# A mixture of 16 experts: sorting the token rows by a scatter, and gathering them by an inverse permutation

## The chip, the core and the metric

The kernel runs on one core of one Trainium2 chip. The metric is the device time of one launch in microseconds (us); several runs are taken and their median is compared. Engines are named as the profile names them: PE is TensorE (PEld its weight loads), ACT ScalarE, DVE VectorE, POOL GpSimd, SP SyncE, which issues most DMA transfers here.

## What is computed

The program is a decoder of four layers on `x` of 4 x 256 tokens by 256 (1024 tokens), with attention, cross attention and an MLP in each. The change lies in the MLP of the third layer, a mixture of 16 experts of which each token takes 4, with a shared expert beside them:

```python
def _L2_ffn_ref(hidden_states, router_w, w_gate, w_up, w_down, sh_gate, sh_up, sh_down, sh_gate_w):
    E, K = (16, 4)
    I_MOE, I_SH = (176, 704)
    h = hidden_states.reshape(-1, orig[-1])          # 1024 x 256
    probs = jax.nn.softmax(h @ router_w.T, axis=-1)
    top_vals, top_idx = jax.lax.top_k(probs, K)
    top_vals = top_vals / jnp.maximum(top_vals.sum(-1, keepdims=True), 1e-09)
    comb = jnp.zeros((N, E), h.dtype).at[jnp.arange(N)[:, None], top_idx].add(top_vals)
    g = jnp.einsum('nh,ehi->eni', h, w_gate)
    u = jnp.einsum('nh,ehi->eni', h, w_up)
    y = jnp.einsum('eni,eih->enh', jax.nn.silu(g) * u, w_down)
    routed = jnp.einsum('enh,ne->nh', y, comb)
    shared = jax.nn.silu(h @ sh_gate) * (h @ sh_up) @ sh_down
    sg = jax.nn.sigmoid(h @ sh_gate_w)
    return routed + sg * shared
```

`h` is the layer-normalised `x`, and the result is added to `x`.

## The kernel before

Tokens lie on 128 partitions in `TT` = 8 tiles, in `X`; features are turned into columns in `HT` for products. The whole stage is the function `experts2`. Each engine has its own program, and semaphores order them; within an engine the order of the source is the order of execution.

**Head.** VectorE and ScalarE normalise (`norm_steps`), writing `HX`, whose rows hold 256 features and 16 more columns. TensorE turns them, multiplies by the router's weights (L2160), and works on the shared expert. That one is cut into six units of 128 hidden columns (`NSH` = 6; the last is half empty), each in two chunks `c` of 512 tokens: `go_up(i, c)` (L2091, gate and up halves), a Silu on ScalarE (L2203), a product on VectorE (`mult`, L2250), `go_down(i, c)` (L2101), which accumulates in four PSUM banks. `FRONT` = 5 units are done ahead of the experts and one behind. Weights of the units come in a ring of four, the last two loaded by SP at L2051.

VectorE meanwhile softmaxes the logits and ranks them. It compares all pairs of the 16 probabilities of a token in `C1` and `C2`, 8 x 16 x 16 = 2048 elements per partition (L2287 to L2294), `RK` is the number of greater ones and `MASK` says `RK` < 4 (L2297). TensorE counts with triangular and all-one matrices how many tokens each expert has before this one (`count`, L2109 to L2114). From the counts come `NB`, the blocks of 128 rows of each expert, `FIRST`, its first block, and `SLOT`, the row of each of the 4 x 8 x 128 token choices in a sorted table (L2327). The number of blocks is fixed at `NBLK` = 47, with padding. `EXPERT` names the expert of each block (L2340).

**Sorting.** POOL scatters the rows of `HX` by `SLOT` into `sorted_rows` in DRAM, in 32 indirect transfers of 128 rows of 1088 bytes (L2379). The table was filled with zeros long before (`late_loads`, L260), so padding rows are zeros. The 16 extra columns carry, per expert, where the result has to go.

**The loop over 47 blocks.** SP loads the 128 rows of block `b` (L2047) and its expert's weights in three transfers, 384, 128 and 64 KB (L2035, L2041, L2043), in rings of four. Its order per block is: rows, a register load of the expert's number, a wait for the up-projection four blocks back, the up weights, a wait for the down-projection four blocks back, the down weights. TensorE runs `turn(b+2)` (two transposes, L2122), `expert_up(b+1)` (six products, L2132) and `expert_down(b)` (two products, L2144). ScalarE copies the turned rows (L2209) and takes the Silu (L2215), VectorE multiplies (`hidden`, L2257 and L2258), finds the destinations from the extra columns (`destination`, L2263 and L2265) and copies the result out of PSUM (`evacuate`, L2271). POOL scatters the result by `DEST` to `chosen` in DRAM, a row for each of the four choices of each token (L2384); rows of padding lie out of bounds and are skipped. In every other block VectorE also quantises a piece of the last layer's ternary weights (`replace`, L2612 and L2613).

**Tail.** The last shared unit; SP loads `chosen` back in 16 transfers (L2075), and VectorE adds the four rows of each token with their weights to `X`, 32 instructions (L2368).

## Time and profile before

| | |
|---|---|
| median of 3 runs | 1313.59 us (1309.03 to 1316.88) |
| the profiled execution | 1310.13 us, span 1308.4 us |
| mean granted TensorE clock | 0.942 |
| TensorE busy | 1129.7 us (86%) |
| VectorE busy | 818.6 us (63%) |
| ScalarE busy | 563.0 us (43%) |
| GpSimd busy | 340.4 us (26%) |
| moved by DMA | 80.83 MB |

A share of busy time is a mean over all stages of the four layers. The stage of the change runs from 805.65 to 1066.4 us of the span, and its own limits are read from the windows and the timeline of that stretch. "Idle before" in a row is the time in which the engine stood, with what released it; a row with xN merges N instructions, and its length runs from the first start to the last end.

### The profile page before, as it was taken

Reading aid. Unit: us, or ns where it says so; the run is one execution under the profiler, and the core shown is the slowest. Engines: PE = TensorE matmul, PEld = TensorE weight load, DVE = VectorE, ACT = ScalarE, POOL = GpSimd, SP = SyncE. Lnnn points to the kernel's source line nnn. Section 1 sums busy time; section 2 is a strip of 40 time slices with the busy share of each in tenths; the row PEclk is TensorE's granted clock in tenths of the full one; section 3 lists DMA queues with packets and bytes.
Section 4 is the critical chain, followed back from the end, with each engine's and each line's share of the span. In section 5 each row is a group of like instructions: output and inputs, shape, how many; then the busy total and the mean of one; then the engine's idle time right before and its main releaser. Section 6 shows DMA issues by size and latency. Waiting matters only on the chain. (4 is left out here: it accounts for less than half of the span.)

```text
span 1308.4 us, 25171 instructions
## 1 busy us (share of the span) xinstructions
PE 1129.7 (86%) x9501; PEld 714.9 (55%) x9516; DVE 818.6 (63%) x2375; ACT 563.0 (43%) x1145; POOL 340.4 (26%) x401
## 2 busy tenths in 40 slices
PE   5888899879999899899999899885888859995898
PEld 3456544447754534456666454555776625663455
DVE  6733487566777444667886674643554376879855
ACT  3667234653434433354443554411222215446443
POOL 2444203100003100145554132073333304451100
PEclk9888899889999899999999999797999969997999
DMA  9000000000074030000000000055888630000000
GB/s 384 3 2 2 1 2 1 1 1 1 1 278 134 1 130 0 1 2 3 3 3 2 2 2 1 13 187 157 263 275 265 186 127 1 2 3 1 1 1 33
DMA packets 44874, 80.83 MB, mean 62 GB/s; under 512 B 5634, under 2 KB 33994, under 8 KB 43985
## 3 DMA queue, kind: packets, MB, share of 16 engines
q1 hardware_dynamic: 40960, 70.55, 16.5%
q0 software_dynamic: 3792, 8.66, 1.8%
q8 instruction: 76, 1.25, 0.4%
q14 instruction: 46, 0.37, 0.1%
HBM read 62.91 MB, written 18.24 MB: 62 GB/s over the span
## 5 line engine op out<-in xcount | busy, mean ns | idle before, releaser
L863 ACT ACTIVATE PT<-PS 128x384 f32<-128x384 f32 (+1 forms) x320 | 153.2, 531 | 185.7 <-PE PS L676 138.2
L272 PE MATMUL PS<-identb 128*128 128x512 bf16 x420 | 106.9, 394 | 19.4 <-PEq L2031 14.8
L796 DVE CUSTOM_DVE_ANT_0 junk<-PS,TRI 128x128 bf16<-128x128 f32 (+1 forms) x384 | 112.7, 353 | 3.9 <-PE PS L657 0.2
L657 PE MATMUL PS<-KS,QM 32*128 32x128 f32 (+1 forms) x768 | 86.7, 347 | 7.5 <-DVE QM L830 6.6
L835 DVE RECIPROCAL OD<-OD 128x256 f32<-128x256 f32 x40 | 69.9, 1747 | 30.9 <-ACT OD L871 25.9
L676 PE MATMUL PS<-QM,KS 32*128 32x256 f32 (+1 forms) x768 | 88.5, 347 | 0.0
L914 POOL TENSOR_TENSOR OD<-OD 128x256 f32<-128x256 f32 x24 | 17.4, 725 | 271.0 <-DVE OD L835 271.0
L904 POOL TENSOR_SCALAR_AFFINE_SELECT PT<-PT 128x512 f32<-128x512 f32 x96 | 60.6, 635 | 98.7 <-ACT PT L863 98.7
L657 PEld LDWEIGHTS PS<-KS,QM 32*128 32x128 f32 x768 | 65.6, 184 | 30.2 <-DVE QM L830 16.6
L272 PEld LDWEIGHTS PS<-identb 128*128 128x128 bf16 x420 | 39.9, 102 | 69.3 <-issue 34.6
L2384 POOL DMA_INDIRECT chosen<-YB,DEST x47 | 48.9, 1040 | 102.7 <-DVE YB L2271 99.9
L745 PE MATMUL PS<-PT,CST 128*32 128x256 f32 (+1 forms) x1280 | 75.4, 353 | 0.0
L2132 PE MATMUL PS<-XT,WE 128*128 128x128 f32 x564 | 72.5, 280 | 0.0
L2132 PEld LDWEIGHTS PS<-XT,WE 128*128 128x128 f32 x564 | 68.5, 196 | 0.4 <-ACT XT L2209 0.4
L676 PEld LDWEIGHTS PS<-QM,KS 32*128 32x128 f32 x768 | 65.6, 184 | 1.9 <-issue 1.2
L1151 POOL TENSOR_TENSOR ROT<-RC,RS 128x512 f32<-128x512 f32 x16 | 20.3, 1270 | 169.6 <-DVE RS L1140 168.3
L745 PE MATMUL PS<-PT,VM 128*32 128x256 f32 (+1 forms) x1024 | 58.3, 345 | 2.0 <-POOL PT L904 1.8
L2257 DVE TENSOR_TENSOR HD<-PS,AE 128x128 f32<-128x128 f32 x47 | 13.7, 291 | 68.1 <-ACT AE L2215 67.8
L1967 DVE SCALAR_TENSOR_TENSOR HB<-HA,ROW,GB 128x512 f32<-128x512 f32 x40 | 30.1, 751 | 40.5 <-ACT HA L1902 36.1
L2122 PE MATMUL PS<-CST,XB 128*128 128x128 f32 x94 | 20.6, 304 | 37.3 <-DMA XB<-sorted_rows 36.9
L2209 ACT ACTIVATE XT<-PS 128x256 f32<-128x256 f32 x47 | 18.0, 383 | 80.7 <-PE PS L2122 80.5
L1902 ACT ACTIVATE HA<-PS,VEC 128x512 f32<-128x512 f32 x42 | 28.7, 687 | 53.5 <-PE PS L1829 53.5
(374 smaller groups left out, 2688.8 us busy)
## 6 DMA issues: line engine op xcount, KB each, us to landing
WE<-w2e_in SPq DMA_DIRECT2D x47, 384.0 KB, 3.9
sorted_rows<-NOTHING SPq DMA_DIRECT2D x1, 6392.0 KB, 35.9
XB<-sorted_rows SPq DMA_DIRECT2D x47, 136.0 KB, 3.7
WE<-w2e_in SPq DMA_DIRECT2D x47, 128.0 KB
WA<-wl_in SPq DMA_DIRECT2D x1, 5137.0 KB, 15.2
GB<-gate_rows SPq DMA_DIRECT2D x8, 512.0 KB, 5.2
WB<-wb_in SPq DMA_DIRECT2D x1, 3208.0 KB, 19.2
WE<-w2e_in SPq DMA_DIRECT2D x47, 64.0 KB
```

The source lines that it names most:

```text
L272: pe.matmul(PS[:, bank, :].rearrange("p (a n) -> p a n", a=4), identb[:], identb[:].rearrange("p (a n) -> p a n", a=1).to_broadcast([P, 4, ...
L657: return pe.matmul(PS[:, s, m * T:m * T + n], queries(U, v)[rows, m * P:(m + 1) * P], keys(U, v)[rows, 0:n], start=True, stop=True, skip_g ...
L676: last = pe.matmul(bank, keys(U, v)[rows, n * P:(n + 1) * P], queries(U, v)[rows, lo:hi], start=n == 0, stop=r > 1, skip_group_check=True, ...
L745: last = pe.matmul(PS[at:at + 32, 7, what * T + lo:what * T + hi], lhs, src, start=what == 0 and v == 0 and n == 0, stop=v == r - 1 and n ...
L796: last = dve.tensor_tensor_reduce(junk[:, s, m * P:m * T + P], PS[:, s, m * T:m * T + (m + 1) * P], TRI[:, (1 - m) * P:T], 1.0, NEG, ALU.a ...
L835: dve.reciprocal(o, o).then_inc(S["at_inv"], 1)
L863: act.activation(PT[:, g % 3, st_slot(k), 0:W], PS[:, st_bank(g, k), 0:W], ACT.Exp, scale=scale).then_inc(S["at_exp"], 1)
L904: pool.affine_select(v, v, [[0, 4], [1, P]], ALU.is_ge, 0.0, base=0, channel_multiplier=-1).then_inc(S["at_masked"], 1)
L1902: act.activation(HA[:, n % 4, :], PS[:, n % 2, :], ACT.Gelu, bias=b).then_inc(S["act_out"], 1)
L1967: ins = dve.scalar_tensor_tensor(HB[:, n % 4, :], HA[:, n % 4, :], gelu_b1[:, f:f + 1], GB[:, owner[f], c * CH:(c + 1) * CH], ALU.subtract ...
L2132: last = pe.matmul(up_bank(b)[:, i * P:(i + 1) * P], WE[:, b % RINGE, (i * KD + k) * P:(i * KD + k + 1) * P], XT[:, b % 2, k * P:(k + 1) * ...
L2384: pool.indirect_dma_start(chosen, bass.IndirectOffsetOnAxis(DEST[:, b:b + 1], 0), YB[:, b % RINGE, :], None, bounds_check=SPARE_ROW - 1, o ...
```

## The change

- **Ranks.** `C1` and `C2` go. The probabilities lie in `PRX`, rows of 16 with four -1 behind. `max` gives the eight largest of a token (8 instructions), the lower four are overwritten by -1, `match_replace` writes -2 where one of the upper four stands (8 instructions), and `MASK` is where the result differs. The four choices of a token are no longer in order of size but of expert: a running sum over `MASK` gives each choice a label from 1 to 32.
- **Inverse permutation.** Slot numbers are split into block and place in the block. `INB` says for each of the 32 choices of a partition in which block it is (32 x 47), `INR` in which place (32 x 128, bf16, in the memory of `RET1`). Two copies of `INB`, multiplied by `code` (POOL) and `row` (ScalarE), are `CODE`. 32 products on TensorE (`locate`) sum `INR` by `CODE`, which gives for each place of each block the number of its row (`DEST`) and of its token (`FROM`).
- **Gather.** SP writes the normalised tokens to `token_rows` in DRAM once. POOL gathers the 128 rows of a block by `FROM`, six blocks ahead (`RINGX`), between its scatters. `sorted_rows`, the 32 scatters, the clearing write and `destination` go.
- **Weights.** One transfer of 576 KB per block, five blocks ahead (`RINGW`). The last 48 hidden rows of an expert lie twice in `HD`, once for each half of the output, so that their down weights fill 128 partitions; `expert_down` has three products and `hidden` three.
- **Order.** `FRONT` is 3 instead of 5. The router's product is cut in two. The ternary sums of ScalarE move into blocks 1 to 12, the scales behind block 17, the replacements to blocks 18 and on. Shared unit 5 has both halves in one PSUM bank, so that its up-projection is half as long.

```diff
-        FRONT = 5
-        COUNT_AT = 1
+        FRONT = 3
+        PAIRS = TT * TOP2
...
                 def _(sp):
-                    for i in range(RING2, NSH):
-                        sp.wait_ge(S["down_ps"], d["down_ps"] + NCH * (i - RING2 + 1))
+                    def weights(b):
+                        e = sp.value_load(EXPERT[0:1, b:b + 1], min_val=0, max_val=E2 - 1)
+                        sp.dma_start(WE[:, b % RINGW, :], w2e[bass.ds(e, 1)].rearrange("a p n -> p (a n)")
+                                     ).then_inc(S[f"weights{b % RINGW}"], 16)
+
+                    for g in range(TT // 2):
+                        norm["tokens"](sp, g)
+                        sp.dma_start(token_rows[2 * g * P:2 * (g + 1) * P, :].rearrange("(t p) n -> p t n", p=P), H[:, 2 * g:2 * g + 2, :]
+                                     ).then_inc(S["rows_kept"], 16)
+                    for i in range(RING2, min(NSH, RING2 + FRONT - 1)):
+                        sp.wait_ge(S["down_ps"], d["down_ps"] + units(i - RING2, NCH - 1))
                         sp.dma_start(W2[:, i % RING2, :], w2s[i]).then_inc(S[f"w_slot{i % RING2}"], 16)
                     sp.wait_ge(S["blocks"], d["blocks"] + 1)
...
-                    for b in range(RINGE, NBLK):
-                        sp.wait_ge(S["turned"], d["turned"] + b - RINGE + 1)
-                        sp.wait_ge(S["row_of"], d["row_of"] + b - RINGE + 1)
-                        rows(b)
-                        e = sp.value_load(EXPERT[0:1, b:b + 1], min_val=0, max_val=E2 - 1)
-                        sp.wait_ge(S["up_ps"], d["up_ps"] + routed(b - RINGE))
-                        up_weights(b, e)
-                        sp.wait_ge(S["down_ps"], d["down_ps"] + routed(b - RINGE))
-                        down_weights(b, e)
+                    for b in range(RINGW):
+                        weights(b)
+                    for b in range(NBLK - RINGW):
+                        sp.wait_ge(S["down_ps"], d["down_ps"] + routed(b))
+                        weights(b + RINGW)
...
+                    def locate(pe):
+                        pe.wait_ge(S["weighed"], d["weighed"] + 1)
+                        pe.wait_ge(S["coded"], d["coded"] + 1)
+                        pe.wait_ge(S["built"], d["built"] + 2)
+                        for j in range(PAIRS):
+                            last = pe.matmul(PS[:, 3, 0:2 * NBLK], INR[:, j, :], CODE[:, j, :], start=j == 0, stop=j == PAIRS - 1)
+                        last.then_inc(S["located"], 1)
...
-                    L(dve.tensor_tensor(C1[:], theirs, mine, ALU.is_gt))
-                    scales(dve, PS[:, 5, :])
-                    L(dve.tensor_tensor(C2[:], theirs, mine, ALU.is_equal))
+                    for t in range(TT):
+                        last = dve.max(TOPV[:, t, :], PRX[:, t, 0:E2])
+                    L(last)
...
+                    for t in range(TT):
+                        last = dve.match_replace(LEFT[:, t, :], TOPV[:, t, :], PRX[:, t, :], -2.0)
...
+                    dve.tensor_tensor(INB[:], WHERE[:, 1].rearrange("p (j b) -> p j b", b=1).to_broadcast([P, PAIRS, NBLK]),
+                                      cst("count")[:, 0:NBLK].rearrange("p (j b) -> p j b", j=1).to_broadcast([P, PAIRS, NBLK]),
+                                      ALU.is_equal).then_inc(S["placed"], 1)
+                    residents(0)
+                    mult(1, 1)
+                    residents(1)
...
                 def _(pool):
-                    pool.memset(HD[:], 0.0)
-                    pool.memset(WE[:, :, UP + D:W2N], 0.0).then_inc(S["blank"], 1)
-                    pool.wait_ge(S["slots"], d["slots"] + 1)
-                    pool.wait_ge(S["rows_clear"], d["rows_clear"] + 16)
-                    for t in range(TT):
-                        for k in range(TOP2):
-                            pool.indirect_dma_start(sorted_rows, bass.IndirectOffsetOnAxis(SLOT[:, t, k:k + 1], 0), HX[:, t, :], None
-                                                    ).then_inc(S["rows_sent"], 16)
+                    def gather(b):
+                        j = b % RINGX
+                        if b >= RINGX:
+                            pool.wait_ge(S["turned"], d["turned"] + b - RINGX + 1)
+                        pool.indirect_dma_start(XB[:, j, :], None, token_rows, bass.IndirectOffsetOnAxis(FROM[:, b:b + 1], 0)
+                                                ).then_inc(S[f"x_slot{j}"], 16)
...
+                    for b in range(RINGX):
+                        gather(b)
                     for b in range(NBLK):
-                        pool.wait_ge(S["row_of"], d["row_of"] + b + 1)
                         pool.wait_ge(S["evacuated"], d["evacuated"] + b + 1)
                         pool.indirect_dma_start(chosen, bass.IndirectOffsetOnAxis(DEST[:, b:b + 1], 0), YB[:, b % RINGE, :], None,
                                                 bounds_check=SPARE_ROW - 1, oob_is_err=False).then_inc(S[f"out_slot{b % RINGE}"], 16)
+                        if b + RINGX < NBLK:
+                            gather(b + RINGX)
```

How TensorE comes from the shared units to the blocks, before (`WA` holds the units' weights, `XB` a block's rows, `WE` its expert's):

```order
L2091 MATMUL PS<-HT,WA 128x512 x4
L2101 MATMUL PS<-WA,MO 128x256 x12
L2122 MATMUL PS<-CST,XB 128x128 x4
L2132 MATMUL PS<-XT,WE 128x128 x6
L2122 MATMUL PS<-CST,XB 128x128 x2
L2132 MATMUL PS<-XT,WE 128x128 x6
L2144 MATMUL PS<-WE,HD 128x256 x2
```

The same place in the changed kernel (`CODE` and `RETA` are the two sides of `locate`):

```order
L2092 MATMUL PS<-WA,MO 128x256 x4
L2122 MATMUL PS<-CODE,RETA 128x94 x32
L2081 MATMUL PS<-HT,WA 128x512 x4
L2092 MATMUL PS<-WA,MO 128x256 x12
L2131 MATMUL PS<-CST,XB 128x128 x4
L2141 MATMUL PS<-XT,WE 128x128 x6
L2131 MATMUL PS<-CST,XB 128x128 x2
L2141 MATMUL PS<-XT,WE 128x128 x6
L2151 MATMUL PS<-WE,HD 128x256
L2154 MATMUL PS<-WE,HD 128x128 x2
```

The 32 products of `locate` stand ahead of the last up-projection of the head, and a block has three down products for two.

POOL in this stage before:

```order
L2371 UNCONDITIONAL_BRANCH
L2373 MEMSET HD 128x512
L2374 MEMSET WE 128x4x256
L2379 DMA sorted_rows<-HX,SLOT 6016x272 x32
L2384 DMA chosen<-YB,DEST 4096x256 x47
```

And in the changed kernel, of which the last two rows repeat to the end:

```order
L2395 UNCONDITIONAL_BRANCH
L2404 MEMSET HD 128x768
L2406 TENSOR_TENSOR CODE<-INB,CST 128x32x47
L2401 DMA XB<-token_rows,FROM 128x256 x6
L2414 DMA chosen<-YB,DEST 4096x256
L2401 DMA XB<-token_rows,FROM 128x256
```

The 32 scatters ahead of the loop have become 47 gathers, six ahead of it and 41 between the scatters of the results.

VectorE from the normalised probabilities to the mask, before, and then in the changed kernel:

```order
L2282 TENSOR_TENSOR PRB<-PRB,ra 128x128
L2287 TENSOR_TENSOR CA<-PRB 128x2048
L2602 TENSOR_REDUCE total<-PS 128x3
L2603 TENSOR_SCALAR SC<-total 128x3
L2604 TENSOR_SCALAR th<-SC 128x3
L2605 TENSOR_SCALAR th<-SC 128x3
L2289 TENSOR_TENSOR CB<-PRB 128x2048
L2250 TENSOR_TENSOR MO<-PS,AO 128x512
L2291 TENSOR_TENSOR CB<-CB,CST 128x2048
L2292 TENSOR_TENSOR CA<-CA,CB 128x2048
L2250 TENSOR_TENSOR MO<-PS,AO 128x512
L2294 TENSOR_REDUCE RK<-CA 128x128
```

```order
L2307 TENSOR_TENSOR PRX<-PRX,ra 128x8x16
L2309 MAX TOPV<-PRX 128x8 x8
L2311 TENSOR_REDUCE rb<-TOPV 128x8
L2312 MEMSET TOPV 128x8x4
L2314 MATCH_REPLACE LEFT<-TOPV,PRX 128x20 x8
L2316 TENSOR_TENSOR MASK<-LEFT,PRX 128x128
```

The mask now stands ahead of the first two products of the shared expert (L2250) instead of behind them.

## Rows read from the trace of the kernel before

**Rows 1.** The stage in windows, core 0: busy us of each engine, clock, DMA share, GB/s

```profile
822.05:850.70 28.65, 23.24 (x76) 12.95 (x77) 22.50 (x40) 10.84 (x22) 0.00 (x0) 0.81 0.04 15
850.70:880.00 29.30, 28.75 (x95) 17.60 (x93) 12.53 (x21) 3.12 (x6) 22.62 (x22) 1.00 0.58 195
880.00:896.00 16.00, 0.00 (x0) 0.00 (x0) 1.15 (x3) 0.00 (x0) 9.60 (x10) 0.63 0.32 114
896.00:1041.10 145.10, 124.06 (x846) 106.16 (x847) 72.30 (x305) 36.01 (x94) 46.90 (x45) 0.98 0.82 248
1041.10:1066.40 25.30, 10.50 (x33) 5.87 (x32) 15.63 (x35) 1.23 (x3) 1.97 (x2) 0.77 0.50 166
```

**Rows 2.** Timeline of the stage's head, VectorE and ScalarE: start, length, engine, line, operation

```profile
822.05 0.30 DVE L2276 COPY LGX<-PS 128x136 f32<-128x136 f32 x1 [9.48 <-PE PS L2160]
822.70 0.29 DVE L2278 TENSOR_TENSOR PRB<-LGX,ra 128x128 f32<-128x128 f32 x1
824.98 0.31 ACT L2221 ACTIVATE PRB<-PRB 128x128 f32<-128x128 f32 x1
826.20 2.29 DVE L2287 TENSOR_TENSOR CA<-PRB 128x2048 f32<-128x2048 f32 x1
840.11 0.22 DVE L2297 TENSOR_SCALAR MASK<-RK 128x128 bf16<-128x128 f32 x1
845.04 0.29 DVE L2305 COPY CNT<-PS 128x128 f32<-128x128 f32 x1 [2.83 <-PE PS L2114]
850.23 0.18 DVE L2327 CAST SLOT<-SLOTF 128x32 uint32<-128x32 f32 x1
```

**Rows 3.** Timeline of the stage's head, TensorE

```profile
817.08 4.93 PE L2160 MATMUL PS<-WA,HT 128*128 128x17 f32 x32 [0.74 <-ACT HT L362]
837.41 1.89 PE L2101 MATMUL PS<-WA,MO 128*128 128x256 f32 x8
839.14 3.60 PE L2091 MATMUL PS<-HT,WA 128*128 128x512 f32 x8
842.57 1.89 PE L2101 MATMUL PS<-WA,MO 128*128 128x256 f32 x8
844.59 0.35 PE L2114 MATMUL PS<-MASK,onesb 128*128 128x16 bf16 x8
```

**Rows 4.** Indirect transfers of line 2379, POOL's last one, and SP behind them

```profile
L2379 POOL DMA_INDIRECT sorted_rows<-HX,SLOT x32: 956/960/1728, 850.7 to 891.4; - x32
891.41 0.96 POOL L2379 DMA_INDIRECT sorted_rows<-HX,SLOT  x1 [0.30 <-issue]
893.85 3.22 SPq L2047 DMA_DIRECT2D XB<-sorted_rows  x5
```

**Rows 5.** Timeline of the block loop, TensorE: the transposes of two blocks

```profile
905.44 0.38 PE L2122 MATMUL PS<-CST,XB 128*128 128x128 f32 x2
907.86 0.38 PE L2122 MATMUL PS<-CST,XB 128*128 128x128 f32 x2
```

**Rows 6.** Groups and sources in the loop: transposes, scatters, landing of the weights

```profile
L2122 PE MATMUL PS<-CST,XB 128*128 128x128 f32 x94 | 20.6, 304 | 37.3 <-DMA XB<-sorted_rows 36.9
L2384 POOL DMA_INDIRECT chosen<-YB,DEST x47: 983/983/1209, 904.9 to 1042.9; - x47
DMA to landing us min/median/max: 3.2/3.9/5.3
```

**Rows 7.** Timeline of a later stage: VectorE's scans with and without POOL's product

```profile
1194.39 2.30 DVE L2432 TENSOR_TENSOR_SCAN PN<-KEEP,EV 128x256 f32<-128x256 f32 x2
1194.75 1.40 POOL L2483 TENSOR_TENSOR NV<-EN,CXT 128x512 f32<-128x512 f32 x1 [17.79 <-ACT EN L2507]
1201.59 1.27 DVE L2432 TENSOR_TENSOR_SCAN PN<-KEEP,EV 128x256 f32<-128x256 f32 x2
```

**Rows 8.** Tail of the stage: a window, and the first addition

```profile
1052.00:1054.00 2.00, 0.00 (x0) 0.00 (x0) 1.93 (x5) 0.00 (x0) 0.00 (x0) 1.00 1.07 378
1051.83 0.88 DVE L2368 SCALAR_TENSOR_TENSOR X<-H,GK,X 128x256 f32<-128x256 f32 x2 [2.32 <-DMA CB<-chosen]
```

354 lines of the change are left out of this document (184 added, 170 removed).

## The prediction, made before the changed kernel was run

> **What bounds the kernel now.** I read the profile in this order: the windows of the second mixture's stage, the timeline of its head, the back-to-back rows of POOL, the groups and timeline of the block loop, then its tail. The stage runs from about 806 to 1066 us, a fifth of the span. The windows [rows 1] are to be read for what is empty: between 880 and 896 us TensorE executes nothing, and its granted clock falls to 0.63. The cause lies earlier. VectorE ranks the 16 probabilities by all pairs, with four 2048-element operations and one reduction of 2.3 us each, so that the mask (L2297) comes at 840.1, 18 us after the logits were copied, and the slots at 850.2 [rows 2]. Then POOL scatters the tokens in 32 indirect transfers, 1.26 us apart, the last starting at 891.4; SP sees them landed at 893.9 and only then loads the first rows of a block [rows 4]. TensorE ran out of its five shared units at 880.
>
> The loop over 47 blocks takes 145.1 us, 3.09 per block, at a clock of 0.98 and a DMA share of 0.82 [rows 1]. A block in which nothing is late takes 2.42 us: transposes start at 905.44 and 907.86 [rows 5]. The rest is waiting; the transposes wait for rows of `sorted_rows` for 36.9 us in all [rows 6]. Those loads are issued behind the weights of the block before, which themselves wait for a down-projection five blocks back, and a transfer here takes 3.9 us from issue to landing [rows 6]. After the loop 25.3 us follow: one shared unit on TensorE, and from 1051.8 on the 32 weighted additions of VectorE [rows 1, 8].
>
> **Part 1, the head of the stage.** The routing product of 4.93 us [rows 3] is cut in two; the first half runs where half a unit ran. Logits come 2.45 us earlier, 819.6 for 822.05. ScalarE no longer has a sum in hand when the exponential is due: the subtraction of 822.70 ended at 823.0 and the exponential started at 824.98 [rows 2]. That gives 1.9 more, so normalised probabilities stand at 821.8. In the place of the pair ranking (13.9 us, 826.20 to 840.11) come eight maxima and eight match-replaces, which the trace does not show. From below they cost 0.15 us each (the small cast takes 0.18 with its start-up [rows 2]), from above 0.29 (a 128-element operation), 2.4 to 4.7 in all. I take 2.4, since they read 16 and 20 elements and are not chained to each other. With a reduction, a fill and the compare (0.75) the mask is there at 824.9, 15.2 us earlier than before.
>
> TensorE's unit 1 up-projection (3.43, from 839.14 to 842.57 [rows 3]) needs the first product, and counting follows it: 829.9. From the count copy to the slots it was 5.2 us [rows 2]; the label compare (0.7) has moved ahead of it and the 256-wide pair product is a 16-element scan. A scan of 256 elements takes 0.64 [rows 7], so the 128-element one is 0.3 to 0.6 and a 16-element one between nothing and 0.6. With a split of the slot into block and place (0.6), `placed` needs about 4.8: 834.7. New are the comparison INB (1504 elements) and two comparisons of 2048. At 2.29 us for 2048 [rows 2] they cost 1.7 + 4.6, with a product of 0.7 between: 841.7.
>
> POOL's CODE product stands beside these. It is 1504 elements, and POOL needs 1.26 to 1.40 us for 512 [rows 7], so 3.7 or more. This row also shows what it does to VectorE: two scans that take 1.27 took 2.30 while POOL's product ran, so they stood still for 1.03 us. POOL starts behind the first INR comparison and holds up the second by about 2.6 us; the bounds are 0 and 3.7. With it: 844.3. The Trainium skill, "SBUF — State Buffer", section "SBUF: two separate sides", has the pair of ports shared by VectorE and GpSimd as an exclusive lock, against a GpSimd operation that reads SBUF also for a two-input VectorE operation. By that rule the second comparison waits for all of CODE; without it the sum would be 2.6 us lower. The row agrees with the lock.
>
> Then 32 bf16 products of 94 columns on TensorE. Eight of 16 columns take 0.35 us [rows 3], so 1.4 at least; at the pace of the f32 pieces of a block (0.11 each) they would be 3.6. I take 2.0, 846.3. Four small VectorE operations give the rows at 847.2. POOL starts gathers then, six of them at 1.26 us, and the first lands 2.5 us after its start (891.4 to 893.9 [rows 4]): 849.7, no longer the last thing. The last is the weights. SP must first load shared chunk 5, behind the down-projection of unit 1, second half. TensorE reaches its end at 846.3 + 3.43 + 1.73 = 851.4 (1.73 from 837.41 to 839.14 [rows 3]). Add 0.4 for that issue, 1.0 for the register load, 3.9 for the landing and 0.6 for the larger size: block 0 starts at 857.3 instead of 896.0. **Term: -38.5 us.** VectorE's 8 additions of the shared part and TensorE's last down-projections lie under it.
>
> **Part 2, the loop.** TensorE's columns are the same; a down-projection has two more instructions, 2.44 us a block for 2.42. VectorE loses the two destination instructions and gains one 64-partition product, about nothing, under TensorE. ScalarE gets 12 sums in blocks 1 to 12; it is busy for 36.0 of the loop's 145.1 us [rows 1] and has room: nothing. SP issues one transfer for four. POOL now makes two indirect transfers per block, the scatter and the gather. The scatter takes 0.98 us in the median [rows 6], and 0.30 from one to the next [rows 4]. If a gather costs what a scatter of rows costs (0.96 + 0.30), POOL needs 2.58 per block, more than TensorE's 2.44. The gather's own price is unknown. Below: it can't make the block shorter than TensorE's 2.44; above, the longest scatter (1.73 + 0.30 [rows 4]) gives 3.3. I take the like price, because that row is the same kind of transfer of the same number of rows. The bytes are 576 KB of weights, 128 gathered and about 87 scattered, 791 for 799: at 2.6 us this is 304 GB/s, and the trace shows 378 at the share of 1.07 [rows 8]. The waits for rows and weights go: a gather is issued six blocks ahead, weights five. I take 2.6 us per block and 1.2 of filling: 123.4 for 145.1. **Term: -21.7 us.**
>
> **Part 3, the tail.** Two shared units move behind the loop, and unit 5 has half its up-projection. A whole up-projection piece is 3.43, a down piece 1.73. On TensorE the last down piece of unit 4 ends after four pieces up, two halves up and four down: 13.7 + 3.4 + 6.9 = 24.0 us. Only then can VectorE form its last product (0.9 with the wait), and the 32 additions stand behind it in its order; from 1051.83 [rows 8] to the stage's end at 1066.4 they took 14.6 us. That makes 39.5 for 25.3. Before, they began 10.7 us after the loop, when the transfers of `chosen` landed. **Term: +14.2 us.** So of the 20.6 us of units taken from the head, most comes back, because nothing covers the additions.
>
> **Part 4, elsewhere.** The clearing write of 6.4 MB and its fill go. They ran beside the cross attention with no row that waits for them: nothing. The constants grow by 60 KB in the initial loads, about 0.2 us: nothing.
>
> **Sum.** -38.5 - 21.7 + 14.2 = -46.0 us. The profiled execution took 1310.1 us, so 1264.1. The median of the runs is 3.5 above it within a scatter of 8; I give 1265.
>
> **The rivals.**
> - The loop runs at TensorE's own rate, 2.44: 115.9 us for the loop, 1257. For it: POOL starts six gathers ahead and may live on them for long. Against it: 2 x 1.26 is more than 2.44. Chance 0.12.
> - The transfers stay the bound: the bytes are the same, the DMA share is 0.82 already, and 3.0 us a block gives 142.2: 1283. Against it: the row at 378 GB/s; for it, that the loop never shows it with weights in the mix. Chance 0.18.
> - The head is late by 10 us, since the weights or the order numbers wait for one more link: 1275. Chance 0.07.
> - POOL is held up by VectorE while it quantises the ternary weights. The scatters of the loop reach 1.21 us for a median of 0.98 [rows 6], those of the head 1.73 for 0.96 [rows 4]. At 0.77 more for each of 24 transfers: 1283. Chance 0.02. The Trainium skill, "SBUF — State Buffer", section "A bandwidth-pool intuition that's wrong", has 620 ns become 3100 under a VectorE copy, which by its figures is an estimate of 60 us over 24 transfers. This trace's 0.23 us does not show it.
> - The other side: a gather costs POOL more than a scatter. From 3.6 us per block on (145.1 and the 24.3 won outside the loop, over 47) the kernel is slower, that is from 2.3 us per gather. At double the scatter's 1.29 it is 3.87 a block, 183.1 for the loop: 1324. Against it: 32 scatters in a row at 1.26. Chance 0.05, 0.04 of it slower and 0.01 in between.
> - That leaves 0.56 for the forecast, whose own range is 1257 to 1273.
>
> **The numbers.** A measurement of this kernel tells from no change what is over about 0.5%, 6.6 us. All cases but the last are beyond it on the fast side, 0.95; within it 0.01; slower 0.04. From the TensorE case with a slightly quicker head to the transfer case with its scatter the range is 1251 to 1288.
>
> **What would show it.** Right: the mask near 825 and the first expert product near 858; no stretch of 10 us without TensorE; blocks 2.6 us apart with POOL busy or starting every 1.3 us; 40 us from the last block to the stage's end. Wrong: transposes waiting for XB with POOL saturated at more than 1.3 us per transfer; expert products waiting for WE with a DMA share of 0.9 or more; a loop of over 142 us.

## The result, and the profile of the changed kernel

| | kernel before | changed kernel |
|---|---|---|
| median of 4 runs each, us | 1311.31 (1308.17 to 1316.88) | 1291.91 (1289.62 to 1293.62) |
| ratio, 95% interval | | 0.9846 [0.9805, 0.9887] |
| first statistics of the stage (its start), us | 805.7 | 799.8 |
| start to first expert product | 91.5 | 50.4 |
| loop: first expert product to the end of the last copy to `YB` | 144.5 | 156.8 |
| from there to the next stage's first addition | 24.7 | 38.9 |

The change is worth 1.5%, 19.4 us; forecast were 46, and 1291.9 lies outside the range of 1251 to 1288. Head and tail came out as forecast. The loop did not get 22 us shorter, it got 12 us longer.

The windows of the changed kernel, with the columns of [rows 1]: the head, the loop, the tail.

```profile
800.00:850.00 50.00, 42.36 (x207) 26.23 (x205) 35.35 (x106) 13.54 (x23) 10.60 (x7) 1.00 0.22 70
850.00:1006.00 156.00, 125.86 (x935) 118.97 (x936) 74.80 (x215) 41.05 (x116) 88.44 (x86) 0.96 0.74 235
1006.00:1046.00 40.00, 28.17 (x94) 16.98 (x93) 18.41 (x40) 3.70 (x7) 1.97 (x2) 0.91 0.34 106
```

In the head TensorE stands still for 3.5 us at most, ahead of the first expert product, and its granted clock is 1.00 against 0.63 to 1.00 in the windows of [rows 1]. The loop is odd: POOL is busy for 88 of 156 us, the DMA share fell from 0.82 to 0.74, TensorE is busy for 81%. Nothing is full, and yet a block takes 3.34 us.

The timeline of the head, VectorE, POOL and TensorE:

```profile
814.42 0.71 DVE L2309 MAX8 TOPV<-PRX 128x8 f32<-128x16 f32 x8
...
816.74 0.29 DVE L2316 TENSOR_TENSOR MASK<-LEFT,PRX 128x128 bf16<-128x128 f32 x1
...
828.36 2.28 DVE L2292 TENSOR_TENSOR RETA<-WHERE,CST 128x2048 bf16<-128x2048 f32 x1
828.52 4.68 POOL L2406 TENSOR_TENSOR CODE<-INB,CST 128x1504 bf16<-128x1504 f32 x1 [28.94 <-DVE INB L2345]
...
831.16 4.19 DVE L2292 TENSOR_TENSOR RETA<-WHERE,CST 128x2048 bf16<-128x2048 f32 x1
...
839.89 1.17 POOL L2401 DMA_INDIRECT XB<-token_rows,FROM  x1 [6.69 <-DVE FROM L2361]
...
850.16 1.89 PE L2141 MATMUL PS<-XT,WE 128*128 128x128 f32 x12 [3.50 <-DMA WE<-w2e_in]
```

The mask stands 16.9 us behind the stage's start where it stood 34.4 behind [rows 2]. The first expert product waits for weights, as the prediction said.

The loop, by its waits (engine, line, releaser: us in total, times, longest):

```profile
ACT AE L2229 <- PE PS L2141: 52.8, 30, 4.9
...
PE PS L2131 <- DMA XB<-token_rows,FROM: 18.9, 13, 2.6
ACT XT L2223 <- remote: 15.5, 10, 3.2
ACT AE L2229 <- remote: 14.4, 5, 3.9
...
DVE YB L2286 <- remote: 7.9, 7, 2.9
```

"remote" is what the profile writes where no instruction that ends just then explains the release. The kernel before has no such row in its whole stage, and its ACT AE row reads 47.8 us in 47 pieces of 2.5 at most. `XT` is filled by ScalarE, which waits there for TensorE's signals alone. What such a wait is, the timeline shows at 860 us:

```profile
860.73 1.50 PE L2141 MATMUL PS<-XT,WE 128*128 128x128 f32 x12
...
862.92 1.01 POOL L2414 DMA_INDIRECT chosen<-YB,DEST  x1 [0.46 <-issue]
...
864.23 0.97 POOL L2401 DMA_INDIRECT XB<-token_rows,FROM  x1 [0.30 <-issue]
...
864.44 1.50 PE L2141 MATMUL PS<-XT,WE 128*128 128x128 f32 x12
866.12 0.38 ACT L2229 ACTIVATE AE<-PS 128x256 f32<-128x256 f32 x1 [3.95 <-PE PS L2141]
...
866.53 0.29 DVE L2276 TENSOR_TENSOR HD<-PS,AE 128x128 f32<-128x128 f32 x1 [4.41 <-ACT AE L2229]
```

The up-projection of a block ends at 862.23 by its row, TensorE goes on to the next block's at 864.44, and ScalarE's gate on the first starts at 866.12, 3.9 us late. VectorE follows ScalarE at once, so that signal is in time. I call these **late signals of TensorE**; whether the signal or the product itself was late the trace can't tell, since ends of matmuls are modelled. The tables below count the "remote" waits of the stage, which is a part of them. In a "remote" wait some of the time can also be an ordinary wait for another engine.

The rows of the timeline give them all, if one takes for each step the time from the end of the last thing that it needs, its own engine included, to its start. In the changed kernel 19 of the 47 gates start over 0.3 us late by this working, 33.3 us in all, 14 copies to `XT` 14.3 us and 6 copies to `YB` 7.8 us. In the kernel before none does. VectorE's products behind ScalarE's gates and TensorE's down-projections behind VectorE's products start within 0.1 us in both kernels and in every run below: only what waits for TensorE is late.

### The profile page after: what moved, and what is told of

Its sections match the earlier page's. It is cut to its first block and busy times, and to the rows that moved or that the text cites. A ratio compares the mean times of both kernels' runs of the same rounds, so it can differ in the third digit from the quotient of the medians.

```text
span 1287.9 us, 24954 instructions
## 1 busy us (share of the span) xinstructions
PE 1118.6 (87%) x9634; PEld 721.2 (56%) x9634; DVE 817.1 (63%) x2307; ACT 561.8 (44%) x1146; POOL 354.3 (28%) x416
## 5 line engine op out<-in xcount | busy, mean ns | idle before, releaser
L653 PEld LDWEIGHTS PS<-KS,QM 32*128 32x128 f32 x768 | 65.5, 184 | 30.3 <-DVE QM L826 16.6
L2141 PE MATMUL PS<-XT,WE 128*128 128x128 f32 x564 | 75.5, 287 | 3.5 <-DMA WE<-w2e_in 3.5
L2141 PEld LDWEIGHTS PS<-XT,WE 128*128 128x128 f32 x564 | 71.3, 203 | 3.8 <-issue 3.7
L1147 POOL TENSOR_TENSOR ROT<-RC,RS 128x512 f32<-128x512 f32 x16 | 20.3, 1272 | 184.5 <-DVE RS L1136 183.2
L2401 POOL DMA_INDIRECT XB<-token_rows,FROM x47 | 47.1, 1003 | 20.7 <-issue 13.1
L741 PEld LDWEIGHTS PS<-PT,CST 128*32 128x32 f32 x1280 | 34.2, 109 | 30.5 <-issue 10.9
```

What stands on the lines that cost most here:

```text
L653: return pe.matmul(PS[:, s, m * T:m * T + n], queries(U, v)[rows, m * P:(m + 1) * P], keys(U, v)[rows, 0:n], start=True, stop=True, skip_g ...
L741: last = pe.matmul(PS[at:at + 32, 7, what * T + lo:what * T + hi], lhs, src, start=what == 0 and v == 0 and n == 0, stop=v == r - 1 and n ...
L2141: last = pe.matmul(up_bank(b)[:, i * P:(i + 1) * P], WE[:, b % RINGW, (i * KD + k) * P:(i * KD + k + 1) * P], XT[:, b % 2, k * P:(k + 1) * ...
L2401: pool.indirect_dma_start(XB[:, j, :], None, token_rows, bass.IndirectOffsetOnAxis(FROM[:, b:b + 1], 0)).then_inc(S[f"x_slot{j}"], 16)
```

## The experiments

The theories at first: W, POOL's wait on a semaphore of TensorE delays its signals; G, the 41 gathers of the loop do; D, the single weight transfer does; P, the down-projection in three products does.

All runs but e12 (four executions) and e18 (five) are single executions. "Loop" is always from the start of the first expert product to the end of the last copy to `YB`, read from the timeline.

| run | time, us | before beside it | loop | "remote" waits |
|---|---|---|---|---|
| changed kernel | 1291.9 | 1311.3 | 156.8 | 37.8 |
| e1 no wait on `turned` | 1287.6 | 1316.0 | 155.0 | 28.3 |
| e2 rows by SP | 1256.0 | 1316.0 | 121.1 | 0 |
| e3 weights in three | 1296.1 | 1316.0 | 158.5 | 42.7 |
| e4 down-projection in two | 1289.2 | 1316.0 | 153.0 | 26.7 |
| e5 scatter by SP | 1271.4 | 1307.6 | 138.3 | 0 |
| e6 plain rows by POOL | 1259.4 | 1307.6 | 127.3 | 0 |
| e7 kernel before, idle gather | 1314.0 | 1307.6 | 145.1 | 0 |
| e8 rows by SP, second scatter | 1261.4 | 1307.6 | 122.3 | 0 |
| e9 spare rows spread | 1295.4 | 1316.5 | 156.1 | 46.6 |
| e10 all from row 0 | 1299.9 | 1316.5 | 162.2 | 43.4 |
| e11 rows by SP, idle gather | 1300.4 | 1314.5 | 161.2 | 24.8 |
| e12 scatter again | 1272.0 | 1314.5 | 116.8 | 29.4, in the head |
| e13 the same, weights later | 1273.5 | 1313.1 | 120.4 | 50.5, in the head |
| e14 e12 with an idle gather | 1316.8 | 1313.1 | 159.1 | 46.7, of it 20.6 in the head |
| e15 e11, every second block | 1266.8 | 1313.1 | 125.2 | 2.6 |
| e16 additions between | 1286.2 | 1313.1 | 157.7 | 26.2 |
| e17 rows of 1088 bytes | 1267.6 | 1313.0 | 136.2 | 0 |
| e18 e17 with e16 | 1262.9 | 1305.7 | 134.5 | 0 |

### Which part of the change costs the loop: e1 to e4

e1:

```diff
-                        if b >= RINGX:
-                            pool.wait_ge(S["turned"], d["turned"] + b - RINGX + 1)
```

> The gather of block b+6 no longer waits on the semaphore turned of TensorE; POOL's wait for the evacuation of block b, which stands before it, already covers it. Nothing of the computation is left out. Theory W (POOL's waiting on a semaphore that TensorE raises delays TensorE's signals): the gates of ScalarE start within 0.1 us of the up-projections again, the loop falls from 156 us to 125 or less, the run to about 1260. Theory G (the gathers themselves, 41 more indirect transfers in the loop, delay them), theory D (the weights' one transfer of 4608-byte rows) and theory P (the down-projection's third product): no difference, loop 154 to 158, run 1288 to 1294.

155.0 us. Theory W falls: the late signals are there without POOL's wait.

e2 (`rows` waits for nothing but its place behind the down-projection):

```diff
-                            gather(b + RINGX)
+                        sp.dma_start(XB[:, j, :], token_rows[at:at + P, :]).then_inc(S[f"x_slot{j}"], 16)
```

> The rows of XB are loaded by SP, 128 rows in a row of token_rows, in place of POOL's indirect gather; which rows belong to a block is left out, so the blocks compute other tokens. Bytes, weights, scatter and all waits of the other engines stay. Theory G (the gathers delay TensorE's signals and land late): the loop falls to 2.44 to 2.6 us a block, 115 to 123 us, the run to 1250 to 1262. Theory D or P: the late signals stay, the loop stays at 150 us or more, the run at 1286 or more. Theory W would also make it fast, and is told apart by the run without the wait.

121.1 us, no late signal, 36 us less for the run. The gathers are the cause, and 2.58 us a block (2.49 in e12) is what the rest of the loop can do, with the single weight transfer and the split down-projection in it.

e3:

```diff
-                        sp.dma_start(WE[:, b % RINGW, :], w2e[bass.ds(e, 1)]...
+                        for lo, hi in ((0, UP), (UP, UP + D), (UP + D, W2N)):
+                            sp.dma_start(WE[:, b % RINGW, lo:hi], w2e[bass.ds(e, 1)]...
```

> The weights of a block come in three transfers again (rows of 3072, 1024 and 512 bytes) on the same semaphore, all on SP. Nothing else changes. Theory D (the 4608-byte rows hold up what runs beside them, the rows of XB and the queues' signals): the loop falls by 10 us or more, to 146 or less, the run to 1281 or less. Theory G, W or P: within 4 us of the changed kernel, or slower by SP's 94 more issues of about 0.05 us each.

e4:

```diff
-                        for k in range(KD):
-                            last = pe.matmul(down_bank(b)[:, k * P:(k + 1) * P], HD[:, b % 2, (k + 1) * P:(k + 2) * P],
+                        last = pe.matmul(down_bank(b), HD[:, b % 2, P:2 * P], WE[:, b % RINGW, UP:UP + D], ...
```

> The down-projection of a block is two products of 256 columns, as before the change, in place of one of 256 and two of 128 columns; the second takes the first's weights, so the second part of the down-projection is computed with the wrong weights and only for half of the columns' inputs. Theory P (the three-part accumulation in one bank delays TensorE's signals): the late signals go, the loop falls to 125 us or less. Theory G, W or D: no difference, 154 to 158 us, and an undisturbed block of 2.42 instead of 2.44 us at most.

158.5 and 153.0 us, the late signals in both: theories D and P fall.

### What about the gather: e5 to e11

Two theories again: K, the gather as such is harmful; N, two indirect transfers a block are, of whatever kind.

e5 (gathers as in e1):

```diff
-                        pool.indirect_dma_start(chosen, bass.IndirectOffsetOnAxis(DEST[:, b:b + 1], 0), YB[:, b % RINGE, :], None,
+                        sp.dma_start(chosen[87 * b:87 * b + n, :], YB[0:n, b % RINGE, :]).then_inc(S[f"out_slot{b % RINGE}"], 16)
```

> The gathers stay, one a block on POOL; the scatter of a block's results is replaced by a store by SP of 87 of its rows in a row of chosen, so which token a row belongs to is left out. POOL makes one indirect transfer a block, as in the kernel before. Theory K (it is the gather as such that delays TensorE's signals and lands late): late signals stay, loop 145 us or more. Theory N (two indirect transfers a block are too many, of whatever kind): the late signals go, the loop is 115 to 125 us, the run 1250 to 1262.

138.3 us, no late signal. It isn't the gather as such; but the loop is still 17 us longer than that of e2, and a block's weights take 8.3 us to land, which I can't explain. By the working above TensorE starts 16 up-projections late there, 11.7 us in all (2.8 of it ahead of block 0), with their turned rows ready: it waits for those weights.

e6:

```diff
-                        pool.indirect_dma_start(XB[:, j, :], None, token_rows, bass.IndirectOffsetOnAxis(FROM[:, b:b + 1], 0)
+                        pool.dma_start(XB[:, j, :], token_rows[b % TT * P:(b % TT + 1) * P, :]
```

> POOL issues the load of a block's rows as a plain transfer of 128 consecutive rows of token_rows, at the place of its gather; which rows belong to a block is left out. Theory K in its narrow form (the indirect addressing costs it): the loop is 115 to 125 us. If every transfer that POOL's software queue writes into SBUF does it: late signals and a loop of 145 us or more. Theory N would, counting only indirect transfers, give 115 to 125 us too.

127.3 us and no late signal: a plain transfer from the same queue doesn't do it.

e7, in the kernel before:

```diff
+                        pool.indirect_dma_start(IDLE[:, b % RINGE, :], None, sorted_rows, bass.IndirectOffsetOnAxis(SLOT[:, b % TT, b % 4:b % 4 + 1], 0)
+                                                ).then_inc(S[f"out_slot{b % RINGE}"], 16)
```

> The kernel before, with one more indirect gather per block (128 rows of sorted_rows to a tile that nobody reads) behind each scatter; nobody waits for it but the reuse of an output slot four blocks later. Theories K and N: late signals appear in the loop, which grows from 144 us to 160 or more, the run from 1311 to 1327 or more. If the delay needed something else of the changed kernel (its single weight transfer, its ring of six): no late signals, run 1311 to 1317.

145.1 us for 144.5: the kernel before bears a gather beside its scatter in each block.

e8, on e2:

```diff
+                        pool.indirect_dma_start(chosen_too, bass.IndirectOffsetOnAxis(DEST[:, b:b + 1], 0), YB[:, b % RINGE, :], None,
```

> As the run with the rows loaded by SP (loop 121.1 us), and each block's results are scattered twice, the second time to a DRAM tensor of its own: two indirect transfers a block and no gather. Theory N: the late signals come back, loop 140 us or more. Theory K: none, loop 121 to 128 us (the 4.2 MB more may cost a little where the DMA share is 0.95).

122.3 us: N falls. It takes a gather and a scatter together, and something that the kernel before doesn't have.

e9 and e10 ask for the addresses (theory A, that many reads of one row do it). In e9 an empty slot fetches the row of its own partition:

```diff
+                    L(dve.tensor_scalar(OWNF[:], ROWF[:], float(SPARE_ROW), cst("row"), ALU.is_equal, ALU.mult))
+                    L(dve.tensor_tensor(OWNF[:], OWNF[:], ROWF[:], ALU.add))
+                    L(dve.tensor_copy(FROM[:], OWNF[:]))
...
```

> Of the 6016 slots 4096 hold a token; in the changed kernel every empty one fetches row 0 of token_rows. Here an empty slot of partition p fetches row p instead, by two more small instructions of VectorE ahead of the gathers (about 0.3 us). Nothing is left out: results of empty slots are dropped by the scatter either way. Theory A (about a third of the gathered rows read one and the same 1 KB of DRAM, and the queues of these transfers stand behind each other there): the late signals and late gathers go, the loop is 120 to 128 us, the run 1256 to 1264. Theory M (a gather of scattered rows between the scatters does it, whatever the addresses): late signals stay, the loop is 150 us or more, the run 1286 to 1294.

In e10 all fetch row 0:

```diff
-                    dve.tensor_scalar(FROM[:], DEST[:], B * T - 1, None, ALU.bitwise_and)
+                    dve.tensor_scalar(FROM[:], DEST[:], 0, None, ALU.bitwise_and)
```

> Every slot fetches row 0 of token_rows, so all blocks compute the same wrong token. Theory A: three times as many reads of one row, the loop grows to 180 us or more and the run to 1320 or more. Theory M: the addresses don't matter, loop 150 to 158, run 1286 to 1294; or, if it is the spread of the addresses that costs, the loop falls to 130 or less.

156.1 and 162.2 us: with no repeated reads by empty slots, or with nothing but one row, the loop is about the same. Theory A falls.

e11, on e2:

```diff
+                        pool.indirect_dma_start(IDLE[:, b % RINGE, :], None, token_rows, bass.IndirectOffsetOnAxis(FROM[:, b:b + 1], 0)
```

> As the run with the rows loaded by SP (which rows belong to a block is left out; loop 121.1 us), and POOL issues the changed kernel's gather behind each scatter all the same, with its own indices, into a tile that nobody reads; only the reuse of an output slot four blocks later waits for it. Theory R (a gather beside a scatter at one pair every 2.6 us is enough; in the kernel before the pairs came every 3.1): late signals come back, loop 145 us or more. Theory C (it needs TensorE to wait for the gather's own landing, so that a gather which is slow beside a scatter holds the loop back and the rest follows): no late signals, loop 121 to 128 us.

161.2 us, against 122.3 with a second scatter in the same place: C falls. Nobody waits for this gather but VectorE's copy to the same slot of `YB` four blocks on, and those copies start 1.5 us late in all. The window from 860 to 970 us of e8, then of e11:

```profile
860.00:970.00 110.00, 107.87 (x866) 104.28 (x866) 71.39 (x202) 40.35 (x111) 80.23 (x81) 0.99 0.98 350
```

```profile
860.00:970.00 110.00, 87.85 (x648) 82.97 (x647) 51.04 (x149) 30.76 (x89) 62.70 (x62) 0.93 0.83 275
```

and POOL's groups in it, in the same order:

```profile
L2423 POOL DMA_INDIRECT chosen<-YB,DEST x41 | 40.6, 991 | 39.2 <-DVE YB L2297 27.8 <-issue 11.4
L2425 POOL DMA_INDIRECT chosen_too<-YB,DEST x40 | 39.6, 990 | 12.2 <-issue 9.4 <-DVE YB L2297 2.7
```

```profile
L2423 POOL DMA_INDIRECT chosen<-YB,DEST x31 | 32.1, 1037 | 60.0 <-DVE YB L2297 52.0 <-issue 8.0
L2425 POOL DMA_INDIRECT IDLE<-token_rows,FROM x31 | 30.9, 997 | 9.4 <-issue 9.1 <-DVE YB L2297 0.3
```

The late signals of e11 in that window:

```profile
ACT AE L2240 <- remote: 11.8, 3, 4.7
ACT XT L2234 <- remote: 4.8, 6, 1.8
```

POOL pays the same for either, 0.99 and 1.00 us. But 41 blocks' scatters go in 110 us with two scatters each, and 31 with a gather that nobody waits for. What the gather costs the loop isn't on its own row; it is on TensorE's consumers: by the working above 16 gates are late by 41.6 us in e11, up to 4.7 each, and none in e8. e8 also tests POOL's sum in the prediction: with two transfers a block POOL, behind its first one, stood 4.5 us of the loop waiting for copies, and a block took 2.60 us for the 2.58 forecast.

### What the kernel before had: pace or rows, e12 to e15 and e17

e12 gives the tokens back to 32 scatters and the rows to SP, and keeps the ranking, the permutation product (for `DEST` alone) and the single weight transfer; `FRONT` is 5:

```diff
+                    for j in range(PAIRS):
+                        pool.indirect_dma_start(sorted_rows, bass.IndirectOffsetOnAxis(SLOT[:, j:j + 1], 0), H[:, j // TOP2, :], None
+                                                ).then_inc(S["rows_sent"], 16)
...
-                        gather(b + RINGX)
+                        sp.dma_start(XB[:, b % RINGX, :], sorted_rows[b * P:(b + 1) * P, :]).then_inc(S[f"x_slot{b % RINGX}"], 16)
```

> The changed kernel without its gathers: the tokens are scattered to sorted_rows by 32 transfers as before the change (no order numbers beside them, the cleared tensor comes back), SP loads a block's rows, the permutation product on TensorE only gives the destinations, its first factor is multiplied on VectorE, and five shared units run ahead of the loop. All is computed. From the runs so far: the scatters go from about 826 to 867 us and land at 869.5, the first block starts at 873 to 875, the loop takes 121 to 126 us as in the run with rows loaded by SP, the tail 25.3 us as before the change: stage end 1020 to 1026 for 1045.9, the run 1265 to 1272. If the loop owes its 157 us to something other than the gathers, 1300.

Four runs gave 1271.96 (1266.89 to 1273.85), ratio 0.9672 [0.9639, 0.9706]. Loop 116.8 us, tail 25.2. The first block came 82.4 us behind the stage's start where the expected 873 to 875 us, counted from a start at 799.8, are 73 to 75. One cause was new to me, late signals in the head, while the scatters ran and no gather existed. The wait, and the timeline of POOL, TensorE and ScalarE in that stretch:

```profile
DVE MO L2283 <- remote: 20.4, 1, 20.4
```

```profile
831.51 2.51 POOL L2422 DMA_INDIRECT sorted_rows<-H,SLOT  x1 [27.39 <-DVE WHERE L2359]
...
857.73 3.60 PE L2093 MATMUL PS<-HT,WA 128*128 128x512 f32 x8
...
860.61 0.60 ACT L2232 ACTIVATE AO<-PS 128x512 f32<-128x512 f32 x1 [8.96 <-remote]
...
861.17 1.89 PE L2104 MATMUL PS<-WA,MO 128*128 128x256 f32 x8
...
874.71 6.12 PE L2093 MATMUL PS<-HT,WA 128*128 128x512 f32 x8 [11.65 <-DVE MO L2283]
```

TensorE stands still for 11.7 us behind a product of VectorE at 873.96. That product had all it needed when ScalarE's Silu ended at 861.21, so 12.7 of its 20.4 us are lateness; the Silu itself came 4.4 us after the up-projection that it waits for. The other cause is in POOL's row: its first four scatters took 1.9 to 2.5 us instead of 0.96 beside VectorE's large comparisons and products, and the last left POOL at 876.9.

e13:

```diff
-                    for b in range(RINGW):
-                        weights(b)
                     sp.wait_ge(S["rows_sent"], 16 * PAIRS)
-                    for b in range(RINGX):
+                    rows(0)
+                    rows(1)
+                    for b in range(RINGW):
+                        weights(b)
+                    for b in range(2, RINGX):
                         rows(b)
```

> The version that scatters the tokens again, with SP loading the first five blocks' weights (2.9 MB) only after the 32 scatters have landed; all is computed. In that version VectorE and ScalarE waited 20.4 and 9.0 us for signals of TensorE that came late while the scatters ran. If the weights' traffic beside the scatters makes the signals late: no such wait of over 1 us, TensorE's front units end by 866, the first block starts at 884 to 888. If the scatters alone do it: waits of 5 us or more remain. The run 1266 to 1274 either way.

The waits remained, 50.5 us in all, so the weights' traffic isn't what makes signals late; the time is that of e12.

e14, on e12 (`RET1` is free in the loop):

```diff
+                        pool.indirect_dma_start(RET1[:, b % RINGE, :], None, sorted_rows, bass.IndirectOffsetOnAxis(SLOT[:, b % PAIRS:b % PAIRS + 1], 0)
```

> The version that scatters the tokens again (loop 116.8 us), with one idle gather a block of 128 rows of sorted_rows by the slots, as the kernel before had in the run that showed no harm; nobody reads it. Theory R (the rate: one gather and one scatter every 2.5 us): late signals in the loop, 140 us or more. Theory T (it depends on what is gathered: token_rows with the repeated indices of the changed kernel, not sorted_rows): no late signals, loop 117 to 125 us.

159.1 us: theory T falls. I took this for the pace, and so reads the expectation of e15, which is e11 with

```diff
+                        if b % 2 == 0:
                             pool.indirect_dma_start(IDLE[:, b % RINGE, :], None, token_rows, ...
```

> The rows by SP (which rows belong to a block is left out; loop 121.1 us without, 161.2 with an idle gather in each block), and the idle gather only in every second block. A price per gather: half the harm, loop 138 to 144 us. A threshold of rate: no late signals, loop 121 to 125 us.

125.2 us, 4 more than without gathers, where every block's costs 40. The harm grows faster than the number of gathers: 9 gates are late here, by 10.3 us, and 16 by 41.6 in e11. But e7 and e14 differ in one more thing, the length of a row: `sorted_rows` has 1088 bytes a row in the kernel before and 1024 in e12 and e14. e17, on the changed kernel:

```diff
+ROWW = D + E2
-    token_rows = nc.dram_tensor("token_rows", [B * T, D], F32, kind="Internal").ap()
+    token_rows = nc.dram_tensor("token_rows", [B * T, ROWW], F32, kind="Internal").ap()
-            XB = tmp("XB", [P, RINGX, D])
+            XB = tmp("XB", [P, RINGX, ROWW])
```

> The changed kernel with token_rows in DRAM rows of 1088 bytes (16 columns of padding, copied from the row's own head), and gathers of 1088 bytes a row, as the rows of sorted_rows were before the change. All is computed. If the row length or its spacing in DRAM makes the gathers harmful: late signals go, the loop is 120 to 130 us, the run 1256 to 1266. If the pace of gathers and scatters does: late signals stay, loop 150 us or more, the run 1286 or more.

136.2 us and not one "remote" row, at a run of 1267.6. I had bet on the pace, and that was wrong: gathers and scatters came closer together here than in the changed kernel (38 gathers in the 110 us below, 32 there). The loop is 6 us above the 130 that I had set as the limit of this case. Its window from 860 to 970 us, POOL's groups in it, and the wait for a gather's rows from 851 to 985:

```profile
860.00:970.00 110.00, 96.90 (x757) 90.67 (x756) 64.39 (x180) 34.98 (x96) 78.09 (x77) 1.00 0.90 288
```

```profile
L2416 POOL DMA_INDIRECT chosen<-YB,DEST x39 | 41.7, 1068 | 20.4 <-issue 11.0 <-DVE YB L2288 9.4
L2403 POOL DMA_INDIRECT XB<-token_rows,FROM x38 | 37.3, 982 | 11.6 <-issue 9.8 <-PE PS L2133 1.5 <-DVE YB L2288 0.3
```

```profile
PE PS L2133 <- DMA XB<-token_rows,FROM: 13.1, 18, 1.6
```

No gate is late; TensorE waits 13.1 us for rows instead. POOL needs 1.07 + 0.98 + 2 x 0.30 = 2.65 us a block, more than TensorE's 2.44, but a block takes 2.90, and POOL stood 9.7 us of the 110 waiting for VectorE's copies: it isn't full. What binds is a chain. The gather of block b+6 stands behind the scatter of block b, and `turn(b+6)` comes three blocks after the down-projection of block b, at 2.44 us a block 7.3 us. From the end of that down-projection VectorE's copy starts 0.5 us later, the gather 2.8 behind the copy's start, and the rows land 5.3 after that (means of the timeline): 8.6 us. In 26 of 40 blocks TensorE starts the transposes within 0.2 us of the landing. The "six blocks ahead" are three. In e6, with 0.5, 2.3 and 4.8, the chain has 7.6 us, and the loop is at 127.3. No run put the gather ahead of the scatter, so this reading of the timeline is not tested by an edit.

### The tail, and the best version: e16 and e18

```diff
                     for i in range(FRONT, NSH):
                         for c in range(NCH):
                             mult(i, c)
-                    for g in range(TT // 2):
+                            if i >= NSH - 2:
+                                add(NCH * (i - NSH + 2) + c)
```

> The changed kernel with VectorE's four groups of weighted additions (3.66 us each) placed behind its products of unit 4, first and second half, and of unit 5, first and second half, in place of all four behind the last product. All is computed. If the additions are uncovered only by their place in VectorE's order: from the loop's end to the stage's end 30 to 32 us for 39.5, the run 7 to 9 us below the changed kernel, apart from what the loop varies by. If the rows of chosen land too late or TensorE's last units are held up by the additions: 37 us or more.

From the last copy to the next stage 29.8 us for 38.9, 9.1 less. The timeline of e16, VectorE: the additions now stand between the products, and the last product is followed by one group, not four.

```profile
1033.85 0.69 DVE L2267 TENSOR_TENSOR MO<-PS,AO 64x512 f32<-64x512 f32 x1
1034.46 0.87 DVE L2389 SCALAR_TENSOR_TENSOR X<-H,GK,X 128x256 f32<-128x256 f32 x2
...
1038.00 0.68 DVE L2267 TENSOR_TENSOR MO<-PS,AO 64x512 f32<-64x512 f32 x1
...
1042.54 0.88 DVE L409 SCALAR_TENSOR_TENSOR X<-PS,SGC,X 128x256 f32<-128x256 f32 x2 [0.32 <-PEq L2037]
```

> The changed kernel with token_rows in rows of 1088 bytes and the additions between the last products; all is computed. If both hold and are independent: loop 132 to 140 us, from its end to the stage's end 29 to 31 us, no late signals, the run 1256 to 1263, a ratio of 0.957 to 0.963 to the kernel before. If the loop's gain was an accident of one execution: 1275 or more.

1262.93 us (1262.03 to 1266.04, five runs) beside 1305.73: ratio 0.9683 [0.9662, 0.9704], a little short of the 0.957 to 0.963 that I expected. Loop 134.5, tail 29.8: both gains hold and add up. It is level with e12 by their ratios, and both are faster than either kernel.

## Why the prediction was right and wrong

- **Part 1, the head, -38.5 us: right.** From the stage's start to the first expert product the change took 41.1 us away. The forecast for the same stretch is 39.9: its 38.5, by its own times 38.7, counts from the first transposes before (896.0) to the first product behind (857.3), and the first product before stood at 897.2. Counted from the stage's start, the mask was 2.3 us earlier than forecast, the comparison `INB` 2.1, the first product 1.2; the weights took 6.0 us from issue (844.17) to the product for 4.5. The maxima and match-replaces together took 2.3 us, from 814.42 to the compare at 816.74, with a reduction and a fill in it; I had taken 2.4 and 0.75. The second comparison with 2048 elements was held by POOL's product for 1.9 us (4.19 for 2.28), forecast 2.6; POOL's product took 4.68 us. The Trainium skill, "SBUF — State Buffer", section "SBUF: two separate sides", had these two locking each other out. The trace agrees for the second comparison; the first began 0.16 us ahead of POOL and lost nothing.
- **Part 2, the loop, -21.7 us: wrong, it was +12.3.** The step that failed is "If a gather costs what a scatter of rows costs", with "The waits for rows and weights go" behind it. As a price on POOL it held: 1.00 us against 1.05 for a scatter (the four terms add to 2.54, not 2.58, which changes nothing in the 2.6 taken). But I counted only POOL's time, bytes and landing. What a gather of 1024-byte rows does to others, beside a scatter in each block, was in no term and in no rival: with it the loop took 161.2 us, with a scatter in its place 122.3. Nor did the waits for rows go: TensorE waited 18.9 us for them in the changed kernel's loop. They had been 20.3 before, since 16.6 of the 36.9 in [rows 6] stand ahead of block 0 and belong to the head. Of the two signs for "wrong" that named a cause neither showed (POOL busy 57%, DMA share 0.74); the third, a loop of over 142 us, did. The loop without gathers takes 121.1 us; that this is near my 123.4 is luck, for POOL makes one transfer a block there and my sum was for two. With two and no late signals, in rows of 1088 bytes, it takes 136.2: the 123.4 holds POOL's pace, but "issued six blocks ahead" was wrong as a lead. The gather stands behind a scatter, so that it is three, and the chain of scatter, gather and landing made TensorE wait 13.1 us for rows there. The 2.5 us that the head's scatters took to land were 5.4 for a gather in the loop.
- **Part 3, the tail, +14.2 us: right**, 38.9 for 24.7. e16 shows the reason given, additions that nothing covers, and that 9 of the 14 were in VectorE's order alone.
- **Part 4, elsewhere, nothing: no run speaks against it.** The stage began 5.9 us earlier in the profile of the changed kernel. In the 18 other profiles the start lies between 798.9 and 800.7 us (6 of them) or between 803.3 and 805.6 (12), and neither the clearing write nor its absence decides it: the versions with it began at 804.4, 798.9 and 803.3 us (e12 to e14), and e9, which is the changed kernel but for three small instructions, at 805.6 with 1295.4 us in all. The kernel before was profiled twice, at 805.7 and 804.2, so that its own spread isn't known.
- The sum: -5.9 - 41.1 + 12.3 + 14.2 = -20.5 us, which is the difference of the profiled executions. The stage alone makes 14.6 of it.
- **The rivals.** That TensorE's own rate would bound the loop was wrong, and so was the transfers' bound: e8 moved 350 GB/s and took 2.6 us a block. The rival in which a gather costs POOL more had the right suspect and the wrong place.

**What stays open** is how late signals arise. Seen are: a gather and a scatter of 1024-byte rows in each block (late), the same with a gather of 1088 bytes (e7, e17, e18: not), with it in every second block (hardly), with two scatters, or a plain load and a scatter (not); and in the head of e12 to e14 scatters alone, of 1024-byte rows every 1.27 us (late), where the kernel before scattered rows of 1088 bytes at the same pace [rows 4] (not). All late cases are dense indirect transfers of 1024-byte rows; but e8 is that as well, and was in time. e10 read one single row and was late, so the spacing of the gathered rows in DRAM is not needed for it. e17 changed the row's length, its spacing in DRAM and the spacing of the tiles in SBUF, and no run took length and SBUF spacing apart; the scatters' rows stayed at 1024 bytes. The Trainium skill, "DMA: Bandwidth & Descriptors", section "Latency and other measured facts", reports DRAM rows spaced by large powers of two as slow for copies from the sync and scalar queues (207 GB/s at 512 KiB, 103 at 4 MiB, 214 being full), and the 4 MiB case as cured by 4 KiB more but not by 192 bytes. That isn't what these runs show: the spacing here is 1 KiB, 64 bytes more cured it, and with a single row read there is no spacing at all. The same page, section "SWDGE vs HWDGE vs iDMA", has GpSimd write its descriptors to rings in SBUF; whether the late signals come from there no run here shows.

## What to carry to other kernels

Price an operation that has not been beside a loop before by an idle copy of it in that loop, not by its own row: the idle gathers made the loop 40 us longer, while their row showed 1.0 us of a POOL that had the time. When no engine and no queue is full and the loop is still slow, look at the gap between a producer's end and its consumer's start. And where work moves behind a loop, look at the order on the engine that comes last: four groups of additions behind the last product cost 9 us that their place between the products gives back.

## What the runs showed of the hardware

- With indirect transfers issued by POOL beside them, TensorE's consumers started late by up to 5.2 us in a loop (e3, a gate) and by 12.7 us in a row of scatters (e12), while what waits for ScalarE or VectorE in the loop started within 0.1 us. With gathered rows of 1088 instead of 1024 bytes (e17, e18) none of these was late.
- A POOL transfer costs POOL 0.94 to 1.08 us on average for 128 rows whether gather or scatter, and 0.57 as a plain load (e6).
- Beside large comparisons on VectorE the first scatters of e12 took 1.9 to 2.5 us for 0.96.
- The program's first 800 us differ by up to 6.8 us among the 20 profiles, in two groups.
